# A gated cross-attention and mixture-of-heads kernel: the second half's opening in another order

## The chip, the cores and the metric

The kernel runs on one core of one Trainium2 chip. A core has TensorE (PE in the profile, its weight loads PEld), VectorE (DVE), ScalarE (ACT), GpSimd (POOL) and SyncE (SP), which here only issues transfers. Each engine runs its own instructions strictly in the order in which the code gives them, and waits on semaphores that the others raise. The metric is the time of one execution on the device in microseconds (us), lower is better.

## The reference, cut to what matters

There are 32 batch entries of 112 tokens with 256 channels. The first half is a cross-attention to 375 context tokens. The second half, where the change lies, is this on the result:

```
x = x + tanh(g_ffn) * ffn(layernorm(x))
q, k   = x Wq, x Wk                       # 16 heads of 64
gate_v = x Ws ; w, sel = top_k(gate_v, 2) # 8 experts for each head
mix_v  = sum_k sigmoid(w) * one_hot(sel)
v      = sum_e mix_v[e] * (x Wv[e])
attn   = softmax(q k^T / 8) v             # per head
gate_o = x Wd ; mask_o = one_hot of its top 2
out    = sum_{h,e} mask_o[h,e] * attn[h] Wo[e]
```

## The kernel before

All of the second half stands in the function `switch`; the work of one batch entry ("a batch" below) is cut into steps, and each engine's block writes out by hand the order of its steps: first an opening for batches 0 to 3, then a loop over `b` in 0..31 in which the steps of several batches interleave, then an end. Nothing but this order and the semaphores decides when a step runs.

The steps that the change and the prediction name, in the order in which a batch's data passes through them:

- DVE `moments_of`, POOL `inverse_deviation` and DVE `normalise_x` make the normalised rows `xn`; there is one buffer, so `normalise_x(b)` waits until PE has transposed batch b-1.
- PE `turn_x(b)` (L976) transposes them into PSUM, ACT `copy_x(b)` (L1154) copies them to `xnT`.
- PE `make_gates(b)` (L982) makes both gates, ACT `copy_gates(b)` (L1159) copies them to the single buffer `gates`. DVE `select_first(b)` finds the best expert (five operations and one that makes `rest`, L1271 to L1282), `select_second(b)` the second best (five operations and the mask, L1289). Every one of these, and two in `weigh_experts`, raises the semaphore `top_step`; a batch has 13 such steps.
- ACT `negated_exp(b)` (L1163), DVE `weigh_experts(b)` (L1295 to L1302): the sigmoid weights, written beside the projections in `pm`.
- PE `make_proj(b)` (L988), ACT `copy_proj(b)` (L1168): the eight experts' value projections into `pm`.
- SP `store_mix(b)`, `load_mix(b)`: `pm` goes to DRAM and comes back in another layout as `pm_te`. POOL `spread_mix(b)` (L1390) builds `mix_bd` from it, PE `mix_values(b)` (L1032) mixes the values, ACT `copy_mixed(b)` (L1194) copies them to `mv`, and SP `store_values(b)`, `load_values(b)` send them through DRAM again to become `v`.
- PE `queries(pair, f)` and `keys(pair, f)` (both L996), f in 0..3, project two batches at a time through one PSUM bank; ACT `copy_queries` (L1175) and `copy_keys` (L1183) empty that bank before the next f. In the loop they are called `fill`.
- PE `scores(b, half)` (L1044), DVE `shift(b, g)` (L1307, L1310), PE `turn` (L1056), ACT `exps`, PE `weigh` (L1068), ACT `copy_attention`, SP `store_attention`, `load_attention`; DVE `invert_sums(b)` (L1316) inverts the row sums that came back, POOL `spread_pick(b)` uses them, PE `sum_heads(b)` (L1078), DVE `copy_sums(b)` (L1322), PE `output(b)` (L1085), DVE `residual(b)` (L1328), SP `store(b)`.

SP's order in the opening, which the change leaves alone, is:

```
for b in range(2):
    store_mix(b)
    load_mix(b)
    if b == 0:
        store_values(0)
        load_values(0)
```

so that the store of batch 1's `pm` is issued only after `load_values(0)`. On PE, `mix_values(0)` and `mix_values(1)` are the last things before the first `turn`.

## Time and profile before

| what | value |
|---|---|
| median of 3 runs | 1341.47 us (1338.84 to 1341.55) |
| profiled execution, its own time | 1340.35 us |
| its span, first to last instruction | 1338.6 us |
| PE busy | 1255.5 us, 94% of the span |
| DVE, ACT, POOL busy | 864.2, 613.2, 551.6 us |
| mean granted clock of TensorE | 0.975 |

The profiled execution's time is 1.75 us above its span. PE is the busiest engine. The second half's block starts at about 667 us with PE idle, its opening lasts to about 726 us and its loop to the end. TensorE's granted clock is given as a share of 2.4 GHz: 1.00 is 2.4 GHz, 0.50 is 1.2 GHz.

### The profile page before, as it was taken

What the parts mean: (1) busy time and instruction counts of PE and PEld (TensorE: products, weight loads), DVE (VectorE), ACT (ScalarE), POOL (GpSimd) and SP (SyncE); (2) the same over time, 40 slices, a digit from 0 to 9 for tenths busy, and PEclk for the clock granted to TensorE, in tenths of its full rate; (3) what the DMA queues carried; (4) which work ended last, traced back from release to release, by engine and by line L of the source; (5) the groups of instructions that cost most, each with busy time, mean ns of one, the idle gap of its engine ahead of it and who ended that gap; (6) DMA issues with size and microseconds to landing.
All of it is one profiled execution on the core that took longest, in us unless ns stands there. A gap on an engine that the chain in (4) does not pass through costs nothing.

```text
span 1338.6 us, 40354 instructions
## 1 busy us (share of the span) xinstructions
PE 1255.5 (94%) x15928; PEld 1020.3 (76%) x15928; DVE 864.2 (65%) x2455; ACT 613.2 (46%) x1353; POOL 551.6 (41%) x823
## 2 busy tenths in 40 slices
PE   5799999999999999999773999999999999999996
PEld 4577787777778777877552888888888888888875
DVE  2566776676667667766425766776677666766651
ACT  3456555655555565555321434444343444334430
POOL 3476667666666766666400122212221222112111
PEclk9899999999999999999996999999999999999996
DMA  8898888768777877776103656665656555656663
GB/s 226 187 196 194 188 198 174 169 161 182 164 162 165 191 156 167 171 167 146 28 18 61 156 138 151 134 145 148 142 138 139 151 139 137 140 147 142 139 142 85
DMA packets 262975, 200.21 MB, mean 150 GB/s; under 512 B 195906, under 2 KB 243844, under 8 KB 258692
## 3 DMA queue, kind: packets, MB, share of 16 engines
q1 hardware_dynamic: 262788, 197.64, 64.5%
q8 instruction: 127, 2.08, 0.7%
q14 instruction: 60, 0.49, 0.1%
HBM read 125.49 MB, written 72.11 MB: 148 GB/s over the span
## 4 chain that ended last, share of the span: by engine, by line
PE 43%; DMA 4%; DVE 1%; ACT 1%; issue 1%; POOL 0%; POOLq 0%; SPq 0%; ACTq 0%; DVEq 0%
PE bank_ab L996 14%; PE bank_ab L988 4%; PE bank_g L1068 4%; PE bank_s L1044 4%; PE bank_ab L1085 4%; PE bank_g L1078 4%; PE bank_t L1056 3%; PE bank_ab L982 2%; PE bank_g L1032 2%; DMA pm_dram<-pm 1%; DMA v_dram<-mv 1%; DMA pm_te<-pm_dram 1%; DMA att_th<-att_dram 1%; PE bank_ab L976 1%; DMA att_dram<-att_q 1%; PE bank_t L1068 1%
## 5 line engine op out<-in xcount | busy, mean ns | idle before, releaser
L753 POOL TENSOR_SCALAR shifted<-raw,neg_max 112x375 f32<-112x375 f32 x512 | 304.7, 603 | 194.7 <-DVE neg_max L646 128.1
L646 DVE CUSTOM_DVE_ANT_0 raw<-bank_s,maskb 112x375 f32<-112x375 f32 x512 | 269.0, 545 | 117.4 <-issue 76.3
L565 ACT ACTIVATE probsT<-bank_t 128x448 f32<-128x448 f32 x384 | 181.1, 546 | 162.7 <-PE bank_t L382 162.7
L382 PE MATMUL bank_t<-ident,shifted 112*128 112x112 f32 x1536 | 170.8, 261 | 2.8 <-POOL shifted L753 2.8
L382 PEld LDWEIGHTS bank_t<-ident,shifted 112*128 112x128 f32 x1536 | 156.2, 141 | 21.5 <-POOL shifted L753 18.6
L373 PE MATMUL bank_s<-K_stack,Q_stack 128*112 128x375 bf16 x512 | 158.6, 337 | 12.4 <-DVE neg_max L646 7.8
L1307 DVE TENSOR_REDUCE max<-bank_s 112x4 f32<-112x448 f32 x128 | 78.8, 616 | 93.9 <-PE bank_s L1044 93.8
L1390 POOL TENSOR_TENSOR mix_bd<-pm_te,tok 128x448 f32<-128x448 f32 x32 | 30.8, 964 | 216.1 <-DMA pm_te<-pm_dram 216.1
L996 PE MATMUL bank_ab<-xnT,wk2T 128*128 128x224 f32 x512 | 109.7, 357 | 2.5 <-ACT kT L1183 1.9
L1379 POOL TENSOR_SCALAR var_eps<-moments 112x1 f32<-112x1 f32 x32 | 7.1, 223 | 254.0 <-DVE moments L1256 254.0
L996 PE MATMUL bank_ab<-xnT,wq2T 128*128 128x224 f32 x512 | 109.6, 357 | 2.3 <-ACT qT L1175 1.9
L996 PEld LDWEIGHTS bank_ab<-xnT,wk2T 128*128 128x128 f32 x512 | 94.1, 190 | 14.0 <-issue 7.4
L996 PEld LDWEIGHTS bank_ab<-xnT,wq2T 128*128 128x128 f32 x512 | 94.2, 190 | 13.7 <-issue 7.4
L396 PE MATMUL bank_o<-probsT,V 128*32 128x112 f32 x3072 | 101.8, 264 | 0.1
L396 PEld LDWEIGHTS bank_o<-probsT,V 128*32 128x32 f32 x3072 | 69.4, 110 | 39.8 <-issue 28.1
L373 PEld LDWEIGHTS bank_s<-K_stack,Q_stack 128*112 128x112 bf16 x512 | 62.7, 130 | 44.2 <-DVE neg_max L646 22.6
L340 PE MATMUL bank_ab<-ctxT,wk_sb 128*128 128x375 f32 x256 | 94.1, 492 | 1.2 <-ACT ctxT L526 1.2
L364 PE MATMUL bank_ab<-wv_sb,ctxT 128*128 128x256 f32 x372 | 90.4, 379 | 0.0
L1310 DVE TENSOR_TENSOR shifted<-bank_s,max 112x448 f32<-112x448 f32 x128 | 80.0, 625 | 4.4
L364 PEld LDWEIGHTS bank_ab<-wv_sb,ctxT 128*128 128x128 f32 x372 | 68.7, 190 | 6.6
L1068 PEld LDWEIGHTS bank_g<-v,probsT 112*64 112x64 f32 (+1 forms) x1792 | 57.8, 131 | 19.7 <-issue 19.7
L1322 DVE COPY uT<-bank_g 128x448 f32<-128x448 f32 x32 | 20.0, 624 | 76.8 <-PE bank_g L1078 76.8
(135 smaller groups left out, 2254.7 us busy)
## 6 DMA issues: line engine op xcount, KB each, us to landing
K_stack<-k_dram SPq DMA_DIRECT2D x64, 562.5 KB, 7.4
k_dram<-k_parts SPq DMA_DIRECT2D x32, 562.5 KB, 4.7
att_dram<-att_q SPq DMA_DIRECT2D x32, 511.0 KB, 4.1
att_th<-att_dram SPq DMA_DIRECT2D x32, 511.0 KB, 4.2
v_dram<-mv SPq DMA_DIRECT2D x32, 455.0 KB, 6.2
v<-v_dram SPq DMA_DIRECT2D x32, 455.0 KB, 4.0
K_stack<-k_dram SPq DMA_DIRECT2D x32, 375.0 KB, 9.4
Q_stack<-q_dram SPq DMA_DIRECT2D x64, 168.0 KB, 9.2
```

The lines of the kernel that those rows point to most:

```text
L340: last = nc.tensor.matmul(bank_ab[:, t, 0:S2], c.wk[:, e, t * P:(t + 1) * P], ctxT[:, p, e, 0:S2], start=(e == 0), stop=(e == EC - 1))
L364: last = nc.tensor.matmul(dst, ctxT[:, p, e, k * KP:(k + 1) * KP], c.wv[:, e, :], start=(e == 0), stop=(e == EC - 1))
L373: nc.tensor.matmul(bank_s[h % 2][0:S, 0:S2], Q_stack[:, p, h, :], K_stack[:, p, h, :], start=True, stop=True).then_inc(scores_ready, 1)
L382: last = nc.tensor.transpose(bank_t[0:KP, k, j * S:(j + 1) * S], shifted[:, g % 2, j, k * KP:(k + 1) * KP], c.ident[0:S, 0:S])
L396: last = nc.tensor.matmul(bank_o[j * VW:(j + 1) * VW, g * S:(g + 1) * S], V[:, p, k, G * g + j, :], probsT[:, g % 2, k, j * S:(j + 1) * S] ...
L565: act.activation(probsT[:, g % 2, k, :], bank_t[0:KP, k, 0:G * S], ACT.Exp).then_inc(exp_done, 1)
L646: dve.tensor_tensor_reduce(raw[:, g % 2, j, :], bank_s[h % 2][0:S, 0:S2], c.maskb[:, :], -1.0, -LEAST, ALU.add, ALU.min, neg_max[:, g % 2, ...
L753: pool.tensor_scalar(shifted[:, g % 2, j, 0:S2], raw[:, g % 2, j, :], -1.0, neg_max[:, g % 2, j:j + 1], ALU.mult, ALU.add).then_inc(shift_ ...
L996: last = nc.tensor.matmul(bank_ab[:, 0, m * 2 * S:(m + 1) * 2 * S], w, xnT[:, e, 2 * h:2 * h + 2, :].rearrange("p r s -> p (r s)"), start= ...
L1068: last = nc.tensor.matmul(weighed(half, m)[lo:hi, :], probsT[:, half, m, lo:hi], v[:, p, 2 * G * half + m, :], start=True, stop=True)
L1307: dve.tensor_reduce(neg_max[:, g % 2, :], sc, AXX, ALU.max).then_inc(max_done, 1)
L1310: dve.tensor_tensor(shifted[:, g % 2, :, :], sc, neg_max[:, g % 2, :].unsqueeze(2).to_broadcast([S, G, S]), ALU.subtract).then_inc(shift_d ...
```

## The change

It writes the second half's opening in another order on PE, ACT, DVE and POOL. On PE the gates of batch 1 come right behind the first projection of queries, the value projections of batches 0 and 1 stand between the other projections, and `scores(0, 0)` and `mix_values(0)` come last; on DVE the whole selection of batch 1 stands ahead of the first `shift`. `copy_gates(b)` no longer waits for all 13 selection steps of batch b-1, but for the six of `select_first(b-1)`. At the very end, DVE inverts the row sums of the last batch ahead of the last but one batch's `residual`. No operation is added or taken away, and SP's order stays.

```diff
@@ -1087,22 +1087,28 @@
 
             turn_x(0)
             make_gates(0)
+            pe.wait_ge(gates_copied, 1)
+            turn_x(1)
+            queries((0, 0), 0)
+            make_gates(1)
+            queries((0, 0), 1)
+            pe.wait_ge(gates_copied, 2)
             make_proj(0)
+            queries((0, 0), 2)
             pe.wait_ge(proj_copied, 1)
-            turn_x(1)
-            for f in range(4):
-                queries((0, 0), f)
-            for f in range(4):
-                keys((0, 0), f)
-            make_gates(1)
             make_proj(1)
+            queries((0, 0), 3)
             pe.wait_ge(proj_copied, 2)
             turn_x(2)
-            scores(0, 0)
+            keys((0, 0), 0)
             make_gates(2)
-            mix_values(0)
+            keys((0, 0), 1)
             pe.wait_ge(gates_copied, 3)
             turn_x(3)
+            scores(0, 0)
+            keys((0, 0), 2)
+            keys((0, 0), 3)
+            mix_values(0)
             for b in range(B):
                 if b + 1 < B:
                     mix_values(b + 1)
@@ -1155,7 +1161,7 @@
 
             def copy_gates(b):
                 act.wait_ge(gates_ready, b + 1)
-                wait(act, top_step, TOP_STEPS * b)
+                wait(act, top_step, TOP_STEPS * (b - 1) + TOP_FIRST)
                 act.activation(gates[:, :, :].rearrange("s g e -> s (g e)"), bank_ab[0:S, 1, 0:2 * H * X], ACT.Copy).then_inc(gates_copied, 1)
 
             def negated_exp(b):
@@ -1210,20 +1216,24 @@
 
             copy_x(0)
             copy_gates(0)
+            copy_x(1)
+            copy_queries((0, 0), 0)
+            copy_gates(1)
+            copy_queries((0, 0), 1)
+            negated_exp(0)
             copy_proj(0)
-            copy_x(1)
-            for f in range(4):
-                copy_queries((0, 0), f)
-            negated_exp(0)
-            for f in range(4):
-                copy_keys((0, 0), f)
-            copy_gates(1)
+            copy_queries((0, 0), 2)
             copy_proj(1)
+            copy_queries((0, 0), 3)
             copy_x(2)
+            copy_keys((0, 0), 0)
+            copy_gates(2)
+            copy_keys((0, 0), 1)
+            copy_x(3)
             negated_exp(1)
-            copy_gates(2)
+            copy_keys((0, 0), 2)
+            copy_keys((0, 0), 3)
             copy_mixed(0)
-            copy_x(3)
             for b in range(B):
                 if b + 1 < B:
                     copy_mixed(b + 1)
@@ -1336,15 +1346,18 @@
                 moments_of(b)
                 normalise_x(b)
             dve.memset(mv[:, :, :, D:W], 1.0).then_inc(ones_set, 1)
-            for b in range(2):
-                select_first(b)
-                select_second(b)
-                weigh_experts(b)
-                moments_of(b + 2)
-                normalise_x(b + 2)
-                if b == 0:
-                    shift(0, 0)
-                    shift(0, 1)
+            select_first(0)
+            select_second(0)
+            moments_of(2)
+            weigh_experts(0)
+            normalise_x(2)
+            moments_of(3)
+            select_first(1)
+            normalise_x(3)
+            select_second(1)
+            weigh_experts(1)
+            shift(0, 0)
+            shift(0, 1)
             select_first(2)
             for b in range(B):
                 if b + 2 < B:
@@ -1364,11 +1377,12 @@
                     shift(b + 1, 1)
                 if b > 0:
                     copy_sums(b - 1)
+                if b + 1 == B:
+                    invert_sums(b)
                 if b + 3 < B:
                     select_first(b + 3)
                 if b > 0:
                     residual(b - 1)
-            invert_sums(B - 1)
             copy_sums(B - 1)
             residual(B - 1)
 
@@ -1403,10 +1417,9 @@
 
             pool.memset(minus_half[:, :], -0.5).then_inc(consts_done, 1)
             pool.wait_ge(consts_done, 2)
-            for b in range(3):
+            for b in range(4):
                 inverse_deviation(b)
             spread_mix(0)
-            inverse_deviation(3)
             spread_mix(1)
             for b in range(B):
                 if b + 4 < B:
```

On PE the opening before, from `make_gates(0)` to `mix_values(1)`. `wq2T` marks queries and `wk2T` keys, four matmuls to each f:

```order
L982 MATMUL bank_ab<-wgT,xnT 112x256 x2
L988 MATMUL bank_ab<-wv2T,xnT 112x512 x2
L976 MATMUL bank_ab<-ident,xn 128x112 x2
L996 MATMUL bank_ab<-xnT,wq2T 128x224 x16
L996 MATMUL bank_ab<-xnT,wk2T 128x224 x16
L982 MATMUL bank_ab<-wgT,xnT 112x256 x2
L988 MATMUL bank_ab<-wv2T,xnT 112x512 x2
L976 MATMUL bank_ab<-ident,xn 128x112 x2
L1044 MATMUL bank_s<-kT,qT 112x112 x8
L982 MATMUL bank_ab<-wgT,xnT 112x256 x2
L1032 MATMUL bank_g<-pm_te,mix_bd 64x64 x28
L976 MATMUL bank_ab<-ident,xn 128x112 x2
```

And the same place of PE after the change, from behind `make_gates(0)` on (`turn_x(1)`); behind the last row shown follow `turn_x(3)`, `scores(0, 0)`, the last two `keys` and `mix_values(0)` and `(1)`:

```order
L976 MATMUL bank_ab<-ident,xn 128x112 x2
L996 MATMUL bank_ab<-xnT,wq2T 128x224 x4
L982 MATMUL bank_ab<-wgT,xnT 112x256 x2
L996 MATMUL bank_ab<-xnT,wq2T 128x224 x4
L988 MATMUL bank_ab<-wv2T,xnT 112x512 x2
L996 MATMUL bank_ab<-xnT,wq2T 128x224 x4
L988 MATMUL bank_ab<-wv2T,xnT 112x512 x2
L996 MATMUL bank_ab<-xnT,wq2T 128x224 x4
L976 MATMUL bank_ab<-ident,xn 128x112 x2
L996 MATMUL bank_ab<-xnT,wk2T 128x224 x4
L982 MATMUL bank_ab<-wgT,xnT 112x256 x2
L996 MATMUL bank_ab<-xnT,wk2T 128x224 x4
```

The gates of batch 1 (the second L982) moved from behind all eight projections to behind the first, and between most projections now stands work on PSUM's other bank.

On ACT, before, from the copies of the keys to the two copies of `copy_mixed(1)`:

```order
L1183 ACTIVATE kT<-bank_ab 128x448 x4
L1159 ACTIVATE gates<-bank_ab 112x256
L1168 ACTIVATE pm<-bank_ab 112x8x64
L1154 ACTIVATE xnT<-bank_ab 128x2x112
L1163 ACTIVATE sig<-best 112x32
L1159 ACTIVATE gates<-bank_ab 112x256
L1194 ACTIVATE mv<-bank_g 128x7x64 x2
L1154 ACTIVATE xnT<-bank_ab 128x2x112
L1194 ACTIVATE mv<-bank_g 128x7x64 x2
```

After the change the same engine, from `copy_x(2)` on (line numbers are six higher there):

```order
L1160 ACTIVATE xnT<-bank_ab 128x2x112
L1189 ACTIVATE kT<-bank_ab 128x448
L1165 ACTIVATE gates<-bank_ab 112x256
L1189 ACTIVATE kT<-bank_ab 128x448
L1160 ACTIVATE xnT<-bank_ab 128x2x112
L1169 ACTIVATE sig<-best 112x32
L1189 ACTIVATE kT<-bank_ab 128x448 x2
L1200 ACTIVATE mv<-bank_g 128x7x64 x4
```

`copy_mixed(0)`, the first two of the `mv` copies, stood right behind `copy_gates(2)`; now five other instructions lie between them, the last two being copies of keys.

On DVE, the last rows of the program after the change (`recip` is `invert_sums`, `uT` is `copy_sums`, `X` is `residual`):

```order
L1326 RECIPROCAL recip<-att_th 128x14
L1332 COPY uT<-bank_g 128x448
L1326 RECIPROCAL recip<-att_th 128x14
L1338 SCALAR_TENSOR_TENSOR X<-bank_ab,tanh_g,X 112x256
L1332 COPY uT<-bank_g 128x448
L1338 SCALAR_TENSOR_TENSOR X<-bank_ab,tanh_g,X 112x256
```

Before, the second `recip` stood behind the first `X`.

## Rows read from the trace of the kernel before

**Rows 1.** Stretches: length, each engine's busy us (instructions), granted clock, DMA share, GB/s

```profile
667.00:704.20 37.20, 26.37 (x162) 17.88 (x162) 11.79 (x41) 7.51 (x16) 3.42 (x8) 0.89 0.06 16
704.20:726.40 22.20, 0.61 (x2) 0.29 (x2) 12.34 (x33) 1.84 (x5) 1.73 (x3) 0.54 0.30 68
...
742.00:1310.00 568.00, 561.63 (x8691) 472.66 (x8689) 387.02 (x904) 230.64 (x533) 113.84 (x144) 1.00 0.61 143
```

**Rows 2.** The chain that ended last, 704 to 730 us: start, us, what

```profile
704.52 0.42 DVE best L1271
...
707.25 0.43 DVE best L1271
...
709.96 0.36 DVE sig L1296
...
710.41 0.38 ACT gates L1159
...
711.74 5.88 DMA v_dram<-mv
...
718.05 4.18 DMA pm_dram<-pm
...
722.25 3.05 DMA pm_te<-pm_dram
...
726.45 1.77 PE bank_g L1032 x56
```

**Rows 3.** Timeline of the opening: start, us, engine, line, operation, [idle before <- releaser]

```profile
673.70 2.80 PE L988 MATMUL bank_ab<-wv2T,xnT 128*112 128x512 f32 x4 [0.47 <-ACT gates L1159]
...
677.18 0.41 PE L976 MATMUL bank_ab<-ident,xn 112*128 112x112 f32 x2 [0.69 <-ACT pm L1168]
...
677.63 0.36 ACT L1154 ACTIVATE xnT<-bank_ab 128x224 f32<-128x224 f32 x1 [0.50 <-PE bank_ab L976]
...
679.86 0.54 ACT L1175 ACTIVATE qT<-bank_ab 128x448 f32<-128x448 f32 x1 [1.87 <-PE bank_ab L996]
...
687.80 0.18 DVE L1295 TENSOR_SCALAR sig<-sig 112x32 f32<-112x32 f32 x1 [8.72 <-ACT sig L1163]
...
689.39 0.30 SPq L912 DMA_DIRECT2D pm_dram<-pm  x1
...
694.94 1.78 PE L996 MATMUL bank_ab<-xnT,wk2T 128*128 128x224 f32 x8 [0.63 <-ACT kT L1183]
695.01 0.93 POOL L1390 TENSOR_TENSOR mix_bd<-pm_te,tok 128x448 f32<-128x448 f32 x1 [4.27 <-DMA pm_te<-pm_dram]
...
696.56 1.03 PE L982 MATMUL bank_ab<-wgT,xnT 128*112 128x256 f32 x4
...
697.62 0.38 ACT L1159 ACTIVATE gates<-bank_ab 112x256 f32<-112x256 f32 x1 [0.32 <-PE bank_ab L982]
...
698.06 1.97 PE L988 MATMUL bank_ab<-wv2T,xnT 128*112 128x512 f32 x4 [0.47 <-ACT gates L1159]
...
701.06 1.04 PE L1044 MATMUL bank_s<-kT,qT 64*112 64x112 f32 x16
...
703.08 1.04 PE L1032 MATMUL bank_g<-pm_te,mix_bd 32*64 32x64 f32 x56
```

**Rows 4.** Short stretches where the granted clock of TensorE changes

```profile
675.00:676.00 1.00, 1.00 (x3) 0.18 (x1) 0.90 (x4) 0.00 (x0) 0.00 (x0) 0.80 0.00 0
726.40:729.90 3.50, 3.45 (x82) 3.37 (x84) 0.00 (x0) 1.59 (x4) 0.00 (x0) 0.50 0.02 5
729.90:731.00 1.10, 1.10 (x13) 0.99 (x12) 0.47 (x1) 0.49 (x2) 0.00 (x0) 0.95 0.67 151
```

**Rows 5.** Timeline of the program's end

```profile
1323.97 0.48 DVE L1328 SCALAR_TENSOR_TENSOR X<-bank_ab,tanh_g,X 112x256 f32<-112x256 f32 x1 [3.91 <-PE bank_ab L1085]
...
1325.30 0.24 DVE L1316 RECIPROCAL recip<-att_th 128x14 f32<-128x14 f32 x1 [0.84 <-DMA att_th<-att_dram]
...
1332.11 3.72 PE L1085 MATMUL bank_ab<-wo2T,uT 128*112 128x256 f32 x8 [0.88 <-DVE uT L1322]
```

More of the change, by code:

```diff
@@ L813, in switch @@
     PW, AW = D + H, W + X
-    TOP_STEPS, TOP_BEST = 13, 7
+    TOP_STEPS, TOP_FIRST, TOP_BEST = 13, 6, 7
     with ExitStack() as ctx:
```

## The prediction

> **What bounds the kernel now.** I read the stretches of the second half first [rows 1]. From 742 to 1310 us PE is busy 561.6 of 568.0 us at a granted clock of 1.00, so the loop is bound by PE's own work, and the change doesn't touch that order. The opening is another matter: from 704.2 to 726.4 us, 22.2 us long, PE does 0.61 us of work. Whatever lets the loop's first step, `mix_values(1)`, start sooner moves everything behind it by the same amount, since all that the loop needs besides is ready long before.
>
> The chain that ended last says what fills the hole [rows 2]. DVE selects batch 1's experts from 704.52 to 710.3 us; then `copy_gates(2)` runs on ACT at 710.41, since it waits for all 13 selection steps; behind it on ACT stands `copy_mixed(0)`, whose PE part was over at 704.12 [rows 3]; its end lets SP issue `store_values(0)` at 711.74. Only behind the load of the same values does SP issue batch 1's `store_mix` (718.05), then the load (722.25), `spread_mix(1)`, and PE starts `mix_values(1)` at 726.45. From the issue at 711.74 to PE's start are 14.71 us, three transfers and a POOL step, all serial. Two things made the start of this tail late: PE's order, which puts gates 1 behind all eight projections, and the two waits on the selection. The timeline also shows DVE idle for 8.72 us before `weigh_experts(0)`, because `negated_exp(0)` stands on ACT behind four copies of queries [rows 3].
>
> **The change, step by step.** No work is added, so the question is when `copy_mixed(0)` ends in the new order; behind it the 14.71 us stay: SP's order is the same, and batch 1's `pm` must still wait its turn.
>
> *PE.* `make_gates(0)` and its copy are as before, so PE is free at 673.70 [rows 3]. There now comes `turn_x(1)`, 0.41 us at the full clock, twice that at the low one: 0.82, end 674.52. ACT's copy takes 0.36, and a hop between engines 0.03 to 0.06 (697.59 to 697.62, 698.00 to 698.06), so the first projection starts at 675.03. Behind it PE has, at the full clock [rows 3]: eight projections of 1.78 (14.24), two gates of 1.03 (2.06), two value projections of 1.97 (3.94), two transposes of 0.41 (0.82), scores 1.04, mixing 1.04: 23.14 us. Where one follows the last without a wait the row's start lies inside the one before (696.56 against 694.94 + 1.78); I take 0.1 for each of 11 such places, an estimate: -1.1. Most of ACT's copies now fall under PE's next work; those that PE still waits for are behind `turn_x(2)` (copy of the fourth queries behind the copy of `pm`, 0.34), before `scores(0, 0)` (0.34) and before the fourth keys (copy 0.54 and two hops, 0.65): 1.33, by walking both queues with these durations. The low clock lasted until about 675.4 (0.80 over 675 to 676 [rows 4]): 0.19. So the mixing ends at 675.03 + 23.14 - 1.1 + 1.33 + 0.19 = 698.6; `copy_mixed(0)`, two instructions that lie within the 1.3 us from 710.41 to 711.74 together with a 0.38 us copy, is over by 699.6 and the store goes at 699.7. That is 12.1 us before 711.74.
>
> *Is all else ready?* DVE: `select_first(0)` starts at 673.7 and both selections of a batch take 5.4 us (704.52 to 709.96 [rows 2]). `negated_exp(0)` now runs at about 680, `weigh_experts(0)` takes 1.5 us (687.80 to 689.39 with the issue [rows 3]), so batch 0's `pm` is stored at about 682.2, when PE's projection of it is copied too. From store to `spread_mix(0)` were 5.62 us (689.39 to 695.01), and 0.93 for that: ready at 688.8, wanted at 697.5, so 8.7 us of cover. `select_first(1)` can start at about 683 and be over by 686, before gates 2 (690). `normalise_x(3)` waits on DVE for `turn_x(2)` on PE (687.0); behind it stand `select_second(1)` and `weigh_experts(1)`, over at 694.6 because of `negated_exp(1)` (692.8). Its `pm` can't be issued before 706, so this has 11 us of cover. The two shifts that the first `turn` needs are over by 697.3, and `select_first(2)` by 700. ACT has 9 us of work in these 25. POOL's `inverse_deviation(3)` ahead of `spread_mix(0)` waits only until 683. Each costs nothing; were its cover gone, it would move the mixing by what is missing.
>
> *The wait of `copy_gates`* inside the loop was met long before and gives nothing there. In the opening it no longer puts the selection ahead of the mixing's copy; that gain is in the 12.1.
>
> *The end.* `invert_sums(31)` waited 0.84 us for its load, landing at 1325.3, while `residual(30)` was over at 1324.45 [rows 5]. Moving it forward can't start it sooner: 0. `residual(30)` moves to about 1325.6; behind it `output(31)` wants it only at 1332.1, a cover of 6 us, and batch 30's store is issued 1.6 us later, long before the last one. Bounds: a gain of at most the residual's 0.48 if the load lands early, no loss.
>
> *The clock.* Here the order may cost something. Before, PE worked from 673.70 without a break when the clock rose. Now 673.70 to 675.03 holds a pair of transposes and then a pause of half a microsecond for ACT's copy. The nearest row for a rise is the loop's start: PE worked without a pause from 726.45, still had 0.50 until 729.9, and 0.95 over the next 1.1 us, so it rose at 730.0, 3.55 us after it began [rows 4]. From 675.03 that gives 678.6. Between 675.4 and 678.6 are 3.2 us at half speed, or 1.6 us lost. Ends: 0 and 1.6. I take 1.6, the row that is most like the place, though in the opening before, the rise came 1.7 us after the pause that ended at 673.70.
>
> The Trainium skill ("TensorE: Matmul & The Clock Gate", section "Part 4: PE-mode transpose") says that a transpose doesn't count as PE being busy in the way that a matmul does for the clock. By that rule `turn_x(1)` would be a gap and the later rise is the likelier; no row here shows a transpose alone raising or not raising it.
>
> *Sum.* 12.1 - 1.6 = 10.5 us. Against the profiled execution's own time: 1340.35 - 10.5 = 1329.85. The median of the runs is 1.12 above that execution, so 1341.47 - 10.5 = 1331.0. At the loop's start PE has now been idle for 15.8 us instead of 22.2 with one transpose in it; it wakes at the low clock as before, and the moment of the rise may fall sooner or later: I allow half of the 3.55 us, which is 1.8 us or 0.9 us of work.
>
> **Rivals.**
> - *The clock rises as early as before.* For it: between 673.70 and 675.4 PE still works 1.2 of 1.7 us, and nothing before 673.70 has changed. The gain is 12.1: 1329.4.
> - *Something in the opening waits that my walk doesn't see*, most likely batch 0's exchange, which needs four engines to meet. It would have to be 8.7 us later before it costs anything; half of the gain left gives 1335.4. Against: each of its parts has microseconds to spare.
> - *The change doesn't do what it says*: the loop's first step is held by something that didn't move, time as before, 1341. Against: each link from 704.52 to 726.45 in the chain follows on the one before without a gap [rows 2].
> - *Slower: the clock stays low through the opening.* The place is PE's stretch from 675.4 to the mixing's end; its 23 us of work would take 46, so the mixing ends near 721 instead of 698.6 and the gain of 12.1 turns into a loss of about 10.5: 1352. It decides from about 24 us of low clock, each worth half. Against: in the old order with more pauses the clock, once up, stayed there; the new stretch is denser (22 of 23.6 us busy).
>
> **How the numbers follow.** Later rise 0.50, early rise 0.31 (together "10 to 12 us gained" 0.81), a partial gain 0.12, no change 0.04, slower 0.03. The time is that of the likeliest, 1331.0. The range takes both clock cases: below 1329.4 - 0.9 - 1.5 for the spread of the runs (2.7 us between three of them), so 1327.0; above 1331.0 + 0.9 + 1.5 and a part of the partial gain, 1334.5. 0.2% is 2.7 us, about what a measurement tells from no change. Faster 0.92, same 0.05, slower 0.03.
>
> **What would show it.** In the changed profile: `mix_values(1)` starts at 714 to 716 instead of 726.45, right behind `spread_mix(1)`; `mix_values(0)` waits for nothing, at about 697.5 to 699; the store of `v` goes at 699.7 to 701.3 and the next `pm` store 6.3 us later; the granted clock tells the 675.4 from the 678.6; the loop is as long as before; the last `recip` still waits for its load. Wrong would be: PE waiting for `mix_bd` at the first mixing, a gap on ACT before `copy_gates(1)`, or a loop that is longer by what the opening gave.

## The result, and the profile after

| | before | changed |
|---|---|---|
| median | 1340.68 us (1338.84 to 1341.55, 4 runs) | 1325.74 us (1323.86 to 1326.26, 4 runs) |
| profiled execution, its own time | 1340.35 us | 1323.86 us |
| its span | 1338.6 us | 1322.1 us |
| mean granted clock | 0.975 | 0.979 |

The ratio is 0.9892, with a 95% interval of 0.9879 to 0.9905: 14.5 us faster, 12.7 to 16.2. The direction was forecast, but the median lies 1.3 us below the lower end of the range.

The stretches of the changed kernel, with the same columns as before:

```profile
667.00:700.00 33.00, 25.99 (x164) 20.05 (x164) 22.25 (x65) 9.13 (x21) 4.59 (x9) 0.83 0.07 18
700.00:713.70 13.70, 0.00 (x0) 0.00 (x0) 1.42 (x4) 0.00 (x0) 0.94 (x1) 0.57 0.47 110
720.00:1296.00 576.00, 571.04 (x8806) 480.18 (x8806) 390.32 (x918) 235.02 (x543) 114.69 (x146) 1.00 0.61 143
1296.00:1322.00 26.00, 15.56 (x220) 12.78 (x218) 5.10 (x10) 3.09 (x8) 4.23 (x4) 0.74 0.31 75
```

The hole in which PE has nothing, 22.2 us in [rows 1], is now the 13.7 us of the second row and a little on either side (15.5 us, from 698.30 to 713.78). In the loop PE is busy 571.0 of 576.0 us, as before. The fourth row holds the end.

The chain that ended last, over the hole:

```profile
697.33 1.02 PE bank_g L1032 x56
...
698.37 0.99 ACT mv L1200 x2
...
699.43 5.74 DMA v_dram<-mv
...
705.61 4.18 DMA pm_dram<-pm
...
709.80 2.83 DMA pm_te<-pm_dram
...
712.70 0.94 POOL mix_bd L1404
...
713.78 1.77 PE bank_g L1032 x56
```

DVE is gone from it. Everything hangs on the end of PE's own opening, and from the issue at 699.43 to `mix_values(1)` at 713.78 are 14.35 us, where 14.71 were assumed from [rows 2].

The opening in the timeline (PE, DVE, SP and POOL rows on which the prediction's walk can be checked):

```profile
672.94 0.63 PE L976 MATMUL bank_ab<-ident,xn 112*128 112x112 f32 x2 [0.47 <-ACT gates L1165]
...
674.02 3.35 PE L996 MATMUL bank_ab<-xnT,wq2T 128*128 128x224 f32 x8 [0.45 <-ACT xnT L1160]
...
678.48 1.68 PE L996 MATMUL bank_ab<-xnT,wq2T 128*128 128x224 f32 x8
...
679.99 1.88 PE L988 MATMUL bank_ab<-wv2T,xnT 128*112 128x512 f32 x4
...
680.88 0.18 DVE L1305 TENSOR_SCALAR sig<-sig 112x32 f32<-112x32 f32 x1 [2.08 <-ACT sig L1169]
...
682.53 0.30 SPq L912 DMA_DIRECT2D pm_dram<-pm  x1
...
688.23 1.17 POOL L1404 TENSOR_TENSOR mix_bd<-pm_te,tok 128x448 f32<-128x448 f32 x1 [3.84 <-DMA pm_te<-pm_dram]
...
693.14 1.78 PE L996 MATMUL bank_ab<-xnT,wk2T 128*128 128x224 f32 x8
...
697.26 1.04 PE L1032 MATMUL bank_g<-pm_te,mix_bd 32*64 32x64 f32 x56
```

`turn_x(1)` took 0.63 us at the low clock, the first projection 3.35, entirely at the low clock; back-to-back steps follow each other in less than their rows' lengths (678.48 to 679.99 is 1.51 us for a row of 1.68). `weigh_experts(0)` waited 2.08 us in place of 8.72 [rows 3]. `spread_mix(0)` is over at 689.40, 7.9 us ahead of `mix_values(0)` at 697.26, which waited for nothing.

Where the granted clock changed:

```profile
677.00:678.00 1.00, 1.00 (x3) 0.72 (x3) 0.90 (x4) 0.54 (x1) 0.00 (x0) 0.50 0.00 0
678.00:679.00 1.00, 1.00 (x6) 0.91 (x5) 0.77 (x3) 0.33 (x1) 0.11 (x1) 0.97 0.00 0
718.00:719.00 1.00, 1.00 (x5) 0.84 (x4) 0.77 (x2) 0.00 (x0) 0.00 (x0) 0.50 0.96 220
719.00:720.00 1.00, 1.00 (x7) 0.96 (x5) 1.00 (x2) 0.00 (x0) 0.00 (x0) 0.99 1.23 141
```

The first rise came at 678.0, where [rows 4] had 675.4; the second at 719.0, 5.2 us after `mix_values(1)`, against 3.55 us.

The end:

```profile
1307.06 3.72 PE L1085 MATMUL bank_ab<-wo2T,uT 128*112 128x256 f32 x8 [0.88 <-DVE uT L1332]
1310.59 0.24 DVE L1326 RECIPROCAL recip<-att_th 128x14 f32<-128x14 f32 x1 [3.67 <-DMA att_th<-att_dram]
1310.82 0.48 DVE L1338 SCALAR_TENSOR_TENSOR X<-bank_ab,tanh_g,X 112x256 f32<-112x256 f32 x1
...
1317.37 1.95 PE L1085 MATMUL bank_ab<-wo2T,uT 128*112 128x256 f32 x8 [0.88 <-DVE uT L1332]
```

The last inversion (1310.59) ran ahead of `residual(30)` (1310.82), as soon as its load was there. `output(31)` took 1.95 us at the full clock, where [rows 5] have 3.72 at the low one.

**Where the 16.5 us between the two profiled executions are.** I cut each execution at four starts: the first DVE instruction of the second half (667.53 before, 666.78 after), `mix_values(1)` (726.45, 713.78), the last `shifted` (1311.91, 1298.47), and the span's end.

| us | first half | opening | loop | end |
|---|---|---|---|---|
| before | 667.5 | 58.9 | 585.5 | 26.7 |
| changed | 666.8 | 47.0 | 584.7 | 23.6 |
| difference | -0.8 | -11.9 | -0.8 | -3.1 |

The first half has the same instructions in both kernels, and the loop differs only in a wait that was long met. So 11.9 us are the opening, and 4.6 us lie where little or nothing was edited (of the end's 3.1, 1.77 are `output(31)` alone). Whether these come from the change was the question for the runs.

### The profile page after: what moved, and what is told of

It is laid out like the page before. It is cut to its first block, busy times and chain, and to the rows that moved or that the text cites. A ratio compares the mean times of both kernels' runs of the same rounds, so it can differ in the third digit from the quotient of the medians.

```text
span 1322.1 us, 40356 instructions
## 1 busy us (share of the span) xinstructions
PE 1252.3 (95%) x15928; PEld 1020.8 (77%) x15928; DVE 862.2 (65%) x2455; ACT 613.0 (46%) x1353; POOL 552.1 (42%) x823
## 3 DMA queue, kind: packets, MB, share of 16 engines
q8 instruction: 127, 2.08, 0.7%
## 4 chain that ended last, share of the span: by engine, by line
PE 45%; DMA 3%; DVE 1%; ACT 1%; issue 0%; POOL 0%; POOLq 0%; SPq 0%; ACTq 0%; DVEq 0%
PE bank_ab L996 15%; PE bank_ab L988 4%; PE bank_g L1068 4%; PE bank_s L1044 4%; PE bank_ab L1085 4%; PE bank_g L1078 4%; PE bank_t L1056 3%; PE bank_ab L982 3%; PE bank_g L1032 2%; DMA v_dram<-mv 1%; PE bank_ab L976 1%; DMA pm_dram<-pm 1%; PE bank_t L1068 1%; DMA pm_te<-pm_dram 0%; DMA att_th<-att_dram 0%
## 5 line engine op out<-in xcount | busy, mean ns | idle before, releaser
L373 PE MATMUL bank_s<-K_stack,Q_stack 128*112 128x375 bf16 x512 | 158.6, 337 | 11.9 <-DVE neg_max L646 7.8
L373 PEld LDWEIGHTS bank_s<-K_stack,Q_stack 128*112 128x112 bf16 x512 | 62.7, 130 | 43.8 <-DVE neg_max L646 22.6
L1189 ACT ACTIVATE kT<-bank_ab 128x448 f32<-128x448 f32 x64 | 34.8, 544 | 74.7 <-PE bank_ab L996 74.7
```

Source lines behind the costliest of these rows:

```text
L373: nc.tensor.matmul(bank_s[h % 2][0:S, 0:S2], Q_stack[:, p, h, :], K_stack[:, p, h, :], start=True, stop=True).then_inc(scores_ready, 1)
```

## The experiments

All the runs below ran on one chip, another than that of the first comparison. The kernel before was run with each group: medians 1343.53 (23 runs, first group), 1344.69 (10 runs, second), 1343.90 (17 runs, third). Its single executions lay between 1340.86 and 1350.54 us. Each kernel was run at least five times, most of them six or twelve. A gain is worked out from the ratio and the median of the kernel before; the plain difference of the two medians is up to 1.7 us smaller. Where two changed kernels are compared "by the ratios", their intervals are about 3 us wide to either side, so only a difference of some 5 us or more is clear of the noise.

**The opening without the end.** The changed kernel with the last inversion back in its old place.

```diff
-                if b + 1 == B:
-                    invert_sums(b)
...
+            invert_sums(B - 1)
             copy_sums(B - 1)
```

> The opening and the wait of copy_gates as changed, the end as before. Theory A (the opening gives all): the same as the changed kernel, 1325.7 us within 1 us, mix_values(1) at 713 to 715 us. Theory B (the inversion moved forward at the end gives 1 us or more, since in the changed kernel's profile the load landed at 1310.57, ahead of the end of output(30) at 1310.78): 1327 us or more. Theory C (the end is faster because TensorE's clock falls and rises at luckier moments, whatever the order): the time is between these, and the end's length, from the last scores to the last instruction, differs between profiles by 1 to 3 us without an edit there.

1331.78 us, ratio 0.9901 (0.9869 to 0.9932): 13.3 us faster than the kernel before on this chip (9.1 to 17.6). Against the changed kernel on the same chip (below, 0.9909) it is not told apart, so the expectation's number of 1325.7 us failed by the chip, while its ratio agrees with theory A; a gain of 1 us at the end couldn't be seen in this interval. The end was 26.2 us long in its profile.

**The end without the opening.** The kernel before with the inversion moved.

```diff
+                if b + 1 == B:
+                    invert_sums(b)
...
-            invert_sums(B - 1)
             copy_sums(B - 1)
```

> The kernel before with the last inversion moved ahead of residual(30) alone. Theory A: no change, 1340.7 us within 0.7 us, the last recip still waits for its load. Theory B: 1 us or more faster, 1339.7 us or less, by the inversion starting right after the load instead of behind output(30) and its residual. Theory C: no change of the median.

1345.51 us, ratio 1.0010 (0.9995 to 1.0026): no change, at most 0.7 us faster. In its profile the load landed at 1326.92 and the inversion ran at once at 1326.94; in the old order it would have stood behind the residual, which there could start at 1326.8 and takes 0.48, so the edit saved 0.3 us of DVE's order. In the changed kernel's profile the residual started at 1310.82 and takes 0.48, against 1310.59, so up to 0.7 us; in the kernel before it is zero, since the load came 0.8 us behind the residual. Theory B is excluded in this order of the opening: 1 us or more isn't there.

**The wait of `copy_gates` alone.**

```diff
-                wait(act, top_step, TOP_STEPS * b)
+                wait(act, top_step, TOP_STEPS * (b - 1) + TOP_FIRST)
```

> The kernel before with only copy_gates waiting for the six steps of select_first(b-1) instead of all 13. In the opening copy_gates(2) could then run at 707.3 instead of 710.4 us and copy_mixed(0) be over by 708.7 instead of 711.7, so if store_values(0) is what the loop waits for, mix_values(1) starts up to 3 us sooner only if batch 1's pm is ready too; that is ready at 711.3 and its store is issued behind load_values(0) at about 715. Theory A: 3.0 us faster, 1337.7 us. Rival: the reordering does all of it and this wait nothing, 1340.7 us.

1342.55 us, ratio 0.9980 (0.9966 to 0.9995): 2.7 us faster (0.7 to 4.6); the medians alone differ by 1.0. In the profile `copy_gates(2)` ran at 707.58, the store of `v` went at 708.90, where the run with the end's edit alone, on the same chip, has 711.66, and `mix_values(1)` started 57.3 us after the half's first DVE instruction, there 60.0. That start, 2.7 us sooner, is theory A's 3 us: in the old order the selection's second half stood in the chain, and this wait put it there. The new order could not be had without it: `copy_gates(1)` would wait for `weigh_experts(0)`, which waits for `negated_exp(0)`, which stands behind it on ACT. That is read from the code; it wasn't tried.

**SP's order too.** The changed kernel, and batch 1's exchange issued ahead of batch 0's values.

```diff
             for b in range(2):
                 store_mix(b)
                 load_mix(b)
-                if b == 0:
-                    store_values(0)
-                    load_values(0)
+            store_values(0)
+            load_values(0)
```

> The changed kernel with SP's opening in another order as well: store_mix and load_mix of batches 0 and 1 first, store_values(0) and load_values(0) behind them. Theory A (the loop's first step waits on batch 1's exchange, which waits only for its turn on SP): pm of batch 1 is ready at 693.9, its exchange takes 7.2 us and spread_mix 1, so PE goes on with mix_values(1) at about 702.5 us instead of 713.8; the values of batch 0 land at about 709.5 and weigh(0, 0) can wait up to 1 us for them: 10 to 11 us faster than the changed kernel, about 1315.5 us. Rival (the values of batch 0 are what the loop waits for in the end, so the hole only moves): less than 5 us faster, 1321 us or more.

1322.62 us, ratio 0.9835 (0.9809 to 0.9860): 22.2 us under the kernel before, 10.0 by the ratios under the changed kernel. `mix_values(1)` started 34.9 us after the half's first DVE instruction, where the changed kernel has 47.0 to 48.5: 12 to 14 us sooner. But the loop's first step, from `mix_values(1)` to `mix_values(2)`, was 21.8 us long, where the kernels with SP's old order have 17.5 to 19.9 (table below). The timeline shows what came back there:

```profile
703.10 1.04 PE L1031 MATMUL bank_g<-pm_te,mix_bd 32*64 32x64 f32 x56 [2.44 <-POOL mix_bd L1403]
...
708.15 0.32 SPq L932 DMA_DIRECT2D v<-v_dram  x1
708.22 0.98 ACT L1199 ACTIVATE mv<-bank_g 128x448 f32<-128x448 f32 x2 [6.51 <-DMA v_dram<-mv]
...
711.85 1.66 PE L1067 MATMUL bank_g<-v,probsT 112*64 112x65 f32 x28 [4.59 <-DMA v<-v_dram]
...
713.66 2.83 PE L987 MATMUL bank_ab<-wv2T,xnT 128*112 128x512 f32 x4
```

`weigh(0, 0)` waited 4.59 us for batch 0's values, whose load was issued only at 708.15; `copy_mixed(1)` waited on ACT for the store of those values, since `mv` is one buffer; and PE came back at the low clock (2.83 us for the value projection, in place of 1.97 [rows 3]). So theory A was right on what opens the loop, and its 10 to 11 us over the changed kernel came about (its 1315.5 us didn't, on this chip), but from an opening that gave 12 to 14 and a first step that took 2 to 4 of them back. The whole loop, at 594.5 us, is within 2 us of the changed kernel's on this chip.

**The changed kernel again.** No edit.

> The changed kernel as it is, to see the gain over more executions, since on this work's second chip those of the kernel before lay between 1340.86 and 1349.08 us. Theory A (the opening is worth 11.9 us, as mix_values(1) starts 11.92 us sooner after the second half's first instruction, and the rest of the first comparison's 14.9 is how single executions differ in loop and end): 11 to 13 us faster than the kernel before. Rival (the order gives 3 us more somewhere behind the opening): 14 us or more faster.

1333.41 us (1327.95 to 1335.18), ratio 0.9909 (0.9883 to 0.9934): 12.2 us faster than the kernel before on this chip (8.9 to 15.7). That is theory A's number, but the interval doesn't exclude the rival's 14. The opening was 48.4 us long, the loop 592.7, the end 25.8. So the loop of the very same kernel was 8.0 us longer than in the first comparison's profile. The transfers of the loop, in the changed kernel's first profile (count, KB each, median us to landing):

```profile
att_th<-att_dram SPq DMA_DIRECT2D x29, 511.0 KB, 4.3
v_dram<-mv SPq DMA_DIRECT2D x29, 455.0 KB, 6.1
...
out_dram<-X SPq DMA_DIRECT2D x29, 112.0 KB, 4.0
```

and in this execution:

```profile
att_th<-att_dram SPq DMA_DIRECT2D x29, 511.0 KB, 5.3
v_dram<-mv SPq DMA_DIRECT2D x29, 455.0 KB, 7.0
...
out_dram<-X SPq DMA_DIRECT2D x29, 112.0 KB, 5.7
```

The same transfers took longer to land here: 7.0 in place of 6.1 us for the store of the values, 5.3 in place of 4.3 for the attention's load. But most of the 8.0 us lie elsewhere. From `mix_values(2)` to `mix_values(31)` the loop took 551.1 us in the first profile and 553.1 in this one, and the first step 17.9 and 19.3; the last step, from `mix_values(31)` to the last `shifted`, is 4.5 us longer. The last step in the first profile and then in this one:

```profile
1282.71:1298.47 15.76, 12.30 (x313) 10.86 (x312) 8.32 (x15) 5.51 (x13) 2.12 (x2) 1.00 0.66 151
```

```profile
1287.43:1307.72 20.29, 15.29 (x313) 12.97 (x312) 8.27 (x16) 5.50 (x13) 2.11 (x2) 0.83 0.64 137
```

The granted clock fell there. The attention's load, issued at 1287.30, was back only at 1294.27; `sum_heads(30)` started 1.7 us later than in the first profile, behind a wait of 1.56 us for POOL, and ran at the low clock (2.89 us in place of 1.78), and `output(30)` behind it too (3.67 in place of 1.95). So one late transfer, and the clock that fell behind PE's wait, make more than half of the difference. That the landing times make the other 3.5 us is argued from these rows; no run isolated it.

**PE kept busy in the hole.** 26 matmuls that nobody reads, ahead of `mix_values(1)`.

```diff
+            def keep_busy(n, keys_done):
+                pe.wait_ge(kk_copied, keys_done)
+                for _ in range(n):
+                    nc.tensor.matmul(bank_ab[:, 0, 0:256], c.wq2T[:, 0, 0:P], c.wq2T[:, 0, 0:256], start=True, stop=True)
...
             for b in range(B):
+                if b == 0:
+                    keep_busy(26, 4)
                 if b + 1 < B:
```

> The changed kernel with 26 matmuls whose result nobody reads (128 rows, 256 columns each, about 0.5 us at the full clock) ahead of mix_values(1), in the 15.5 us in which PE waits for batch 1's exchange. Theory A (the loop's start is slow only because the clock fell in the hole): the granted clock is 1.00 at mix_values(1), the next 5 us of work pass in half the time, 2.6 us faster than the changed kernel. Rival (what follows is bound by the exchange of batch 2, not by PE): 1 us faster or less.

1332.33 us, ratio 0.9900 (0.9872 to 0.9927): not told from the changed kernel. The edit missed its aim. The matmuls took 11.49 us in place of the 13 that I had worked out, and left a gap:

```profile
698.48 11.49 PE L1091 MATMUL bank_ab<-wq2T 128*128 128x256 f32 x52
...
714.85 1.77 PE L1032 MATMUL bank_g<-pm_te,mix_bd 32*64 32x64 f32 x56 [4.87 <-POOL mix_bd L1411]
```

```profile
698.00:712.00 14.00, 11.97 (x92) 10.23 (x81) 3.49 (x9) 1.15 (x3) 0.00 (x0) 1.00 0.41 89
712.00:713.00 1.00, 0.00 (x0) 0.00 (x0) 0.00 (x0) 0.00 (x0) 0.00 (x0) 0.73 1.03 255
713.00:718.00 5.00, 3.15 (x79) 3.07 (x81) 0.00 (x0) 1.29 (x3) 0.93 (x1) 0.50 0.02 4
```

The clock fell at 712.5, within the 4.9 us of gap, and was low when the loop began, so neither theory was tested. The run stands as one more of the changed opening.

**PE kept busy at the end.** 17 such matmuls in the end's waits.

```diff
+                if b + 1 == B:
+                    keep_busy(2, 2 * B)
                 turn(b, 1)
...
+                if b + 1 == B:
+                    keep_busy(2, 2 * B)
                 weigh(b, 1)
+                if b + 1 == B:
+                    keep_busy(1, 2 * B)
...
+                    if b + 1 == B:
+                        keep_busy(1, 2 * B)
                     output(b - 1)
+            keep_busy(10, 2 * B)
             sum_heads(B - 1)
             pe.wait_ge(out_done, B - 1)
+            keep_busy(1, 2 * B)
             output(B - 1)
```

> The changed kernel with 17 such matmuls in the end's waits of PE (2, 2, 1, 1, 10 and 1 of them ahead of the last turn, the last weigh, the last two sum_heads and outputs). Theory A (the end's length goes by where the clock falls and rises in its pauses): the end, from the last shifted to the last instruction, is 20 to 21 us instead of 23.6 to 27.5, at a clock of 1.00, and differs little between executions; 4 to 5 us faster than the changed kernel. Rival (the end goes by its transfers, about 8 us for the last exchange, and PE's clock is worth under 2 us).

1331.00 us, ratio 0.9887 (0.9863 to 0.9912), 2.4 us by the medians under the changed kernel, with intervals that overlap. The end was 23.5 us long, 2.3 less than the 25.8 of the changed kernel on this chip, and not the 20 to 21 expected: the clock still fell once, at 1309.3 us, behind the 1.8 us in which PE had waited for POOL. The end's length thus goes in part by the clock: with these matmuls it was 23.5 us here and 22.6 in the next run, in the other kernels 23.6 to 27.5. The 3.1 us that the first comparison's end gave are a like amount, and there `output(31)` alone ran 1.77 us shorter (1.95 against 3.72). Whether that is chance or follows from the inversion, which let PE's last pause be shorter (2.52 us ahead of the last `sum_heads`, 4.09 in the kernel before), no run isolated; the run with the end alone had 2.90 us of pause and its `output(31)` still took 3.73.

**SP's order, the hole and the end together.** The edits of three runs above, with 4 matmuls in the hole.

> The changed kernel with SP's opening order of the run with batch 1's exchange first, 4 of the unread matmuls ahead of mix_values(1) and the 17 at the end. Theory A: the three gains add up to 8 to 11 us over the changed kernel, about 21 to 24 us under the kernel before. Rival (the loop gives back what its earlier start brings, as its first steps then wait for batch 0's values): no faster than the run with the 17 matmuls alone.

1321.03 us, ratio 0.9824 (0.9793 to 0.9855): 23.7 us under the kernel before, 11.4 by the ratios under the changed kernel. Theory A's sum, at its upper end, and the rival is excluded (it would have been no faster than 0.9887). It isn't told from the kernel with SP's order alone (0.9835), so what the unread matmuls add stays open.

**The mixing earlier.** The changed kernel with `mix_values(0)` and `copy_mixed(0)` ahead of the last two keys and their copies.

```diff
             scores(0, 0)
+            mix_values(0)
             keys((0, 0), 2)
             keys((0, 0), 3)
-            mix_values(0)
...
             negated_exp(1)
+            copy_mixed(0)
             copy_keys((0, 0), 2)
             copy_keys((0, 0), 3)
-            copy_mixed(0)
```

> The changed kernel with mix_values(0) ahead of the last two keys on PE, and copy_mixed(0) ahead of their copies on ACT. In the changed kernel's profile spread_mix(0) is over at 689.4 us, scores(0, 0) at 693.2, and mix_values(0) starts only at 697.26. Theory A (the loop's first step comes 14.4 us after the store of batch 0's values, whenever that is): the store goes at 695.2 instead of 699.43, mix_values(1) starts 4.2 us sooner, 42.8 to 44 us after the second half's first DVE instruction instead of 47.0 to 48.4, and the time is 4 us less than the changed kernel's. Rival (PE's or ACT's own work in the opening takes the place of the transfers): under 1 us.

1326.73 us, ratio 0.9868 (0.9840 to 0.9897): 17.7 us under the kernel before, 5.5 by the ratios under the changed kernel, whose interval (0.9883 to 0.9934) this one just overlaps.

```profile
691.25 1.04 PE L1032 MATMUL bank_g<-pm_te,mix_bd 32*64 32x64 f32 x56
...
693.42 0.38 SPq L926 DMA_DIRECT2D v_dram<-mv  x1
...
700.07 0.37 SPq L912 DMA_DIRECT2D pm_dram<-pm  x1
...
708.52 1.77 PE L1032 MATMUL bank_g<-pm_te,mix_bd 32*64 32x64 f32 x56 [12.10 <-POOL mix_bd L1404]
```

The first DVE instruction of the half is at 664.86 here, so `mix_values(1)` starts 43.7 us after it, as forecast (42.8 to 44). The changed kernel on this chip, whose half begins at 666.61, has:

```profile
700.10 0.38 SPq L926 DMA_DIRECT2D v_dram<-mv  x1
...
715.02 1.77 PE L1032 MATMUL bank_g<-pm_te,mix_bd 32*64 32x64 f32 x56 [16.04 <-POOL mix_bd L1404]
```

The store goes 28.6 us after the half's first instruction in place of 33.5, and `mix_values(1)` 43.7 in place of 48.4: 4.9 and 4.7 us sooner. These two profiles show the prediction's main step: what counts in the opening is when batch 0's values leave ACT, and the rest is a tail of transfers. The time agrees with it, within its noise.

**The mixing earlier, and SP's order.** The same, with SP's opening written out:

```diff
+            store_mix(0)
+            load_mix(0)
+            store_mix(1)
+            store_values(0)
+            load_mix(1)
+            load_values(0)
```

> The same, and SP's opening order store_mix(0), load_mix(0), store_mix(1), store_values(0), load_mix(1), load_values(0). Theory A: batch 1's exchange goes out at 694 us and its spread is over at 702, mix_values(1) starts 35 to 37 us after the second half's first instruction; batch 0's values are back by 706 and weigh(0, 0), due at 709, no longer waits for them as it did for 4.6 us in the run with SP's order alone. 11 to 13 us faster than the changed kernel, 23 to 25 under the kernel before. Rival (the loop gives back 4 to 6 us as in that run, whatever the values do, by its transfers colliding): 7 us faster than the changed kernel or less.

1321.08 us, ratio 0.9818 (0.9795 to 0.9841): 24.5 us under the kernel before, 12.2 by the ratios under the changed kernel, as theory A said. `mix_values(1)` came 37.9 us after the half's first DVE instruction, up to 3 later than forecast: batch 1's load, issued at 698.13 while the store of the values was under way, fed `spread_mix(1)` only at 704.37, 6.2 us later, where the changed kernel takes 2.9 (709.80 to 712.70) and the run before this one 3.1. `weigh(0, 0)` ran at 712.16 without a wait. The loop's first step was 18.1 us long, so nothing came back there. The kernel is level with the one of SP's order and the busy matmuls (0.9824, the intervals overlap almost wholly), and unlike that one it does no useless work.

**SP's order in the kernel before.**

```diff
             for b in range(2):
                 store_mix(b)
                 load_mix(b)
-                if b == 0:
-                    store_values(0)
-                    load_values(0)
+            store_values(0)
+            load_values(0)
```

> The kernel before with only SP's opening order changed (batch 1's exchange ahead of batch 0's values). Batch 1's pm is ready at 711.3 us there. Theory A (in the old order the hole was two things in a row, the late selection and batch 1's exchange behind batch 0's values): the exchange goes out at 711.4 instead of 718.05, mix_values(1) starts at 719.8 instead of 726.45, 52.3 us after the second half's first instruction instead of 58.9, 6.6 us faster than before. Rival (batch 0's values, now behind it, hold weigh(0, 0) and take the gain back): 2 us faster or less.

1340.42 us, ratio 0.9963 (0.9944 to 0.9982): 5.0 us faster (2.4 to 7.5). `mix_values(1)` came 51.7 us after the half's first DVE instruction, 8.3 sooner than in the run with the end's edit alone (60.0). The loop's first step was 21.0 us long against 17.8 there, as `copy_mixed(1)` waited 7.53 us on ACT for the store of batch 0's values, so `mix_values(2)` was 5.1 us sooner. Both theories had a part: the exchange behind the values was 8.3 of the old hole's 22.2 us, and the values behind the exchange take about 3 back. The loop as a whole was 595.2 us long against 588.0; another 5.4 of these lie in its last step, at a clock of 0.77.

The cuts of all profiled executions, made as above, with the loop's first step (`mix_values(1)` to `mix_values(2)`) and its last (`mix_values(31)` to the last `shifted`):

| us | opening | loop | its first step | its last step | end |
|---|---|---|---|---|---|
| *old order of the opening* | | | | | |
| before (first chip) | 58.9 | 585.5 | 17.6 | 16.9 | 26.7 |
| end alone | 60.0 | 588.0 | 17.8 | 16.7 | 25.7 |
| wait alone | 57.3 | 587.1 | 17.5 | 16.4 | 27.5 |
| old order with SP's | 51.7 | 595.2 | 21.0 | 22.1 | 26.5 |
| *new order* | | | | | |
| changed (first chip) | 47.0 | 584.7 | 17.9 | 15.8 | 23.6 |
| changed again | 48.4 | 592.7 | 19.3 | 20.3 | 25.8 |
| without the end | 47.7 | 587.9 | 17.8 | 16.2 | 26.2 |
| busy hole | 47.9 | 591.6 | 18.3 | 18.0 | 25.6 |
| busy end | 48.5 | 589.0 | 19.9 | 16.8 | 23.5 |
| SP's order too | 34.9 | 594.5 | 21.8 | 18.0 | 26.3 |
| SP's order, hole and end | 33.3 | 592.5 | 22.9 | 15.7 | 22.6 |
| mixing earlier | 43.7 | 586.3 | 17.9 | 16.0 | 26.1 |
| mixing earlier, SP's order | 37.9 | 591.8 | 18.1 | 18.1 | 25.4 |

On the second chip the opening is 60.0 in the old order and 47.7 to 48.5, on average 48.1, in the new one: 11.9 us, as on the first. The loop of one and the same kernel differs by 8.0 us. The ends without the inversion's edit are 26.2 to 27.5 us long, those with it and no unread matmuls 23.6 to 26.3, on average 1.2 us shorter; the run with the end alone allows 0.7 of that, and the rest isn't told from the spread.

## Why the prediction was wrong in size, point by point

- **What bounds the kernel** held: the hole before the loop's first step, filled by the late end of `copy_mixed(0)` and 14.7 us of transfers. Moving the store of batch 0's values 4.9 us forward moved the loop's start by 4.7 and the time by 5.5, the last with an uncertainty nearly as large.
- **The walk of PE's opening** was right in its order and its waits. It was mis-sized by 1.4 us: 10.5 forecast, 11.9 measured. Too dear were: the step up to the first projection, 1.08 us and not 1.33, mainly as the transposes at the low clock took 0.63 and not 0.82 (0.2); steps that follow each other, which overlap by 0.16 to 0.20 us at ten places and 0.06 at two, not by 0.1 at eleven (0.7), and whose rows are then shorter than the prices (1.68 for 1.78, 1.88 for 1.97, 0.36 for 0.41; 0.6); and the exchange, 14.35 in place of 14.71 (0.4). Too cheap were PE's three remaining waits, 1.6 in place of 1.33 (0.3), and the low clock, 2.0 in place of 1.8 (0.2). Together that is the 1.4. Two of these could be read before: the prediction's own example (696.56 against 694.94 + 1.78) gives an overlap of 0.16, and the trace of the kernel before has a pair of transposes at the low clock:

```profile
670.10 0.63 PE L976 MATMUL bank_ab<-ident,xn 112*128 112x112 f32 x2 [3.41 <-DVE xn L1263]
```

- **The clock in the opening.** Of the two cases the later rise came, at 678.0, as chosen (678.6, less the 0.75 by which the half began sooner, is 677.85). That the order causes it is likely and not certain: in the nine profiles with the new order the rise came 9.9 to 13.2 us after the half's first DVE instruction, in the four with the old one 7.9 to 10.4. These overlap, and the 7.9 of the kernel before is the earliest of all, so that a part of the case's being right is luck.
- **"Each costs nothing"** held for batch 0's exchange (7.9 us of cover; 8.7 were worked out), the wait on `turn_x(2)` and the selections.
- **The wait of `copy_gates`** was rightly counted inside the 12.1; alone it is worth 2.7 us.
- **The end** at zero held within 0.7 us for the edit, and the median shows nothing. The stated bound of "at most 0.48" was passed by 0.2, as an inversion behind the residual would also have waited for the residual's start, 0.23 us after the load. The measured end was 3.1 us shorter all the same, mostly by PE's clock.
- **The clock at the loop's start**: the allowance was 0.9 us either way; the rise came 5.2 us after PE's first work and not 3.55, a loss of 0.8.
- **The failed step** is a matter of two sizes, not of the mechanism. The median came 5.3 us under the forecast 1331.0. Of these, 1.4 are the sum's term for the opening, mis-sized as above (10.5, measured 11.9); 0.8 are the kernel before, whose median with a fourth run is 1340.68 and not 1341.47; and 3.0 lie outside the opening, where the sum had nothing. The range should have held such things, but its "1.5 for the spread of the runs (2.7 us between three of them)" took three executions that lay close together for the spread of all. On the second chip the kernel before was between 1340.86 and 1350.54 us, and the changed one moved by 7 us. In the profiled pair the part outside the opening lay in the first half (0.8), the loop (0.8) and the end (3.1). Repeated on the second chip the same kernel gained 12.2 us (8.9 to 15.7), and the kernels without the end's edit and with the busy hole gained 13.3 and 13.4. So no 3 us more are shown to belong to the order, nor are they excluded; the intervals of both comparisons overlap between 12.7 and 15.7. Why four executions on the first chip all lay to the fast side stays open; the small number of them and the end's clock are what the traces offer.
- **The rivals**: the early clock (12.1) didn't occur in the changed kernel, the partial gain and the slower case neither. Its 12.1 is nearer to the measured 11.9 than the chosen 10.5, but not because the clock rose early.

The Trainium skill's rule on transposes and the clock ("TensorE: Matmul & The Clock Gate", section "Part 4: PE-mode transpose") agrees with what was seen here, in that the rise came later with `turn_x(1)` in the place of a matmul; but the pauses around it changed too and the two groups overlap (9.9 to 13.2 us against 7.9 to 10.4), and no run changed that transpose alone, so it isn't shown.

## What to carry to other kernels

When a loop is bound by one engine and its first step hangs on a chain of transfers, find the last instruction that the chain waits for and walk the queues of all engines to it: each microsecond by which it comes sooner is about a microsecond of the whole (4.9 us for 4.7 here). Then look at the issuing queue itself, whose order was worth 10 us more in the new order of the engines and 5 in the old one, but check what the displaced transfer feeds next, since 2 to 4 us came back there. And take the width of a range from how single executions differ where the code is the same, cut by stretch, not from three medians that happen to agree.

## What the runs showed of the hardware

- One program's stretches without any edit differed much more between executions than its total had let expect: a loop of 584.7 and 592.7 us for the same kernel, with the median landing of a 455 KB store at 6.1 and 7.0 us. 4.5 of the 8.0 us lay in the loop's last step, where a load was late, PE waited 1.56 us, and the granted clock was 0.83 over the step in place of 1.00.
- TensorE's granted clock fell at 712.5 us after 11.5 us of dense work and a gap that had begun only at 710.0 (run with the busy hole), and the loop then began at 1.2 GHz just as after 15 us of pause. A filler that stopped 4.9 us short of the next work was worth nothing that could be measured.
- A load issued while a store of the same queue was under way took 6.2 us to its reader in place of 2.9 (mixing earlier with SP's order; the load came 1.2 us behind the store). Where the load was issued 0.5 us ahead of the store (SP's order in the kernel before, 714.79 and 715.26), its reader started after 3.4 us. So exchanges that are laid over each other don't always keep their single prices.
